# Routing streamed with the base weights in 274-column passes, x2 split straight from PSUM, a new order of the LayerNorm work in the down loop and behind it

## The chip, the cores and the metric

The kernel runs on one core of a Trainium2 chip. The metric is the device time of one execution in microseconds (us). Work is spread over five engines that each run their own instruction list in order: TensorE (PE in the rows; its weight loads are PEld), VectorE (DVE), ScalarE (ACT), GpSimd (POOL) and SyncE (SP), which here issues DMA transfers. Engines wait for each other through semaphores.

## The reference

One decoder layer over 8 sequences of 128 tokens with 512 features. The part that the change touches is the last one: a down projection, a LayerNorm, attention over a context, a LayerNorm, a mixture of four LoRA experts and a last LayerNorm. Mamba mixing and the gate and up projections come before it and stay as they are.

```python
h = h + mamba2(rmsnorm(h))                     # not touched
hid = silu(n @ gate_w.T) * (n @ up_w.T)        # n = rmsnorm(h), 1792 wide
x1 = layernorm(h + hid @ down_w.T)             # LayerNorm 0, "u1"
a  = softmax(x1 @ ctx.T) @ ctx
x2 = layernorm(x1 + a)                         # LayerNorm 1, "u2"
logits = x2 @ gate.T + expert_bias             # 4 experts
e = argmax(logits)
y = x2 @ W_up + (x2 @ lora_A[e].T) @ lora_B[e].T
out = layernorm(x2 + y)                        # LayerNorm 2, "u3"
```

## The kernel before

A tile is one sequence of 128 tokens, so there are 8 tiles. Products that need near-float32 accuracy run as three passes of rounded float32 ("fp32r"): each operand is split in a high part (a rounding copy) and a low part (operand minus high part), and `three_pass` multiplies high by low, high by high and low by high. Its three matmuls are lines L582 to L584 in the rows. Matmuls on plain float32 operands show as two instructions each.

The last stage is a software pipeline, `tail(t)`, written out by hand on each engine. In `tail(t)` TensorE computes the down projection of tile t (14 blocks of three passes, `down`, cut in segments by `SEGS`), and between the segments it serves tile t-1 (transposing u1 in `turn_x1`, scores in `attend`, transposing the softmax in `turn_ex`, `mix` with the context) and tile t-2 (transposing u2 in `turn_x2`, `route`, `base`, `turn_z`, `lora`). `route` multiplies x2 by 36 columns (4 gate columns and 4 x 8 LoRA columns) in plain float32; `base` multiplies it by the 512 columns of W_up, 4 blocks of three 512-column passes; `lora` adds the chosen expert's product into the same bank of PSUM.

VectorE in `tail(t)` adds u1 of tile t-1 and takes its moments, does the same for u3 of tile t-3, normalises both, splits x2 of tile t-2, takes the row maximum of the scores, computes the low part of the next tile's hidden rows (`split_hid`, 1792 columns), picks the expert (`route`, eight small instructions that depend on each other), and forms and normalises u2. ScalarE copies the transposes from PSUM, makes the high part of the hidden rows, the exponentials, and the two small steps (`rstd`) between moments and normalising. The order on each engine is the order of the code. Tiles 0 to 2 run from straight code, tiles 3 to 6 in a loop with two tiles a round, and tile 7 (`last`) in an order of its own with `END_SEGS`, behind which tiles 5, 6 and 7 drain.

Down, loop and end wait for these semaphores: `hid_lo` (low part of hidden rows there), `q_ok` (x1 transposed and copied), `x2_lo`, `ex_ok`, `zm_ok`, `zmT_ok`, `ln_out` and `route_ps`.

## Time and profile before

| what | value |
|---|---|
| median of 3 runs | 414.51 us (412.84, 414.51, 414.68) |
| the profiled execution | 412.89 us |
| its span, first to last instruction | 411.2 us |
| TensorE busy | 97% of the span |
| VectorE, ScalarE busy | 71%, 46% |
| mean granted TensorE clock | 0.992 of full |

The span is the stretch that the rows below are timed in, from 0 at its start. The profiled execution's own time is 1.69 us longer than the span. Of the three runs one is at the profiled execution's time and two are 1.6 to 1.8 us above it.

### The profile page before, as it was taken

To read this page: it belongs to the slowest core of one execution; us is meant where nothing else is said; L and a number is where in the kernel's file an instruction comes from. 1 tells how busy PE (TensorE), PEld (TensorE's weight loads), DVE (VectorE), ACT (ScalarE), POOL (GpSimd) and SP (SyncE) were. 2 spreads that over 40 slices of the span, in tenths; PEclk is the share of its full clock that TensorE was granted. 3 is DMA by queue.
4 is the path that set the end of the run, shared out by engine and by line. 5 is a ranking of instruction groups with operands and counts; after the bars stand their busy time and mean duration, and the time that the engine had idled before them with its cause. 6 is when DMAs were issued, how large, how long until landed. Compare 5 with 4: busy or idle time off the path is not lost.

```text
span 411.2 us, 5381 instructions
## 1 busy us (share of the span) xinstructions
PE 398.0 (97%) x1932; PEld 318.5 (77%) x1936; DVE 290.3 (71%) x517; ACT 190.0 (46%) x383; POOL 131.6 (32%) x117
## 2 busy tenths in 40 slices
PE   7999999999999999999999999999999999999984
PEld 3878887766669997888888888887888788787753
DVE  3496991146886689889897989695567657675676
ACT  6668745736655555443515242863314133142131
POOL 3404225614424663565564737740000000000000
PEclk9899999999999999999999999999999999999998
DMA  7901111010000105111112031352110120110002
GB/s 248 316 2 52 53 51 51 2 51 2 0 1 2 52 2 205 53 51 53 51 51 68 36 102 52 110 184 66 51 53 26 52 78 26 51 47 29 28 0 77
DMA packets 11659, 25.52 MB, mean 62 GB/s; under 512 B 1681, under 2 KB 1809, under 8 KB 11634
## 3 DMA queue, kind: packets, MB, share of 16 engines
q1 hardware_dynamic: 10482, 23.10, 16.9%
q10 hardware_dynamic: 1152, 2.10, 1.4%
q8 instruction: 14, 0.23, 0.2%
q14 instruction: 11, 0.09, 0.1%
HBM read 23.10 MB, written 2.10 MB: 61 GB/s over the span
## 4 chain that ended last, share of the span: by engine, by line
PE 85%; DVE 7%; ACT 3%; POOL 2%; issue 2%; ACTq 0%; DVEq 0%; POOLq 0%
PE bank L582 23%; PE bank L584 23%; PE bank L583 23%; PE bank L653 2%; PE bank L707 2%; PE bank L640 2%; PE bank L847 2%; PE bank L858 1%; PE bank L593 1%; PE bank L869 1%; POOL sets L501 1%; PE bank L621 1%; DVE tmp L1668 1%; PE bank L662 1%; DVE big L1459 1%
## 5 line engine op out<-in xcount | busy, mean ns | idle before, releaser
L582 PE MATMUL bank<-sets,station 128*128 128x512 f32 (+1 forms) x424 | 164.1, 387 | 1.1 <-DVE station L1549 0.7
L584 PE MATMUL bank<-sets,station 128*128 128x512 f32 (+1 forms) x424 | 158.5, 374 | 0.0
L583 PE MATMUL bank<-sets,station 128*128 128x512 f32 (+1 forms) x424 | 158.3, 373 | 0.0
L582 PEld LDWEIGHTS bank<-sets,station 128*128 128x128 f32 x424 | 80.0, 189 | 18.6 <-issue 3.6
L583 PEld LDWEIGHTS bank<-sets,station 128*128 128x128 f32 x424 | 80.0, 189 | 15.3 <-issue 2.2
L584 PEld LDWEIGHTS bank<-sets,station 128*128 128x128 f32 x424 | 79.8, 188 | 14.4
L540 POOL TENSOR_TENSOR big<-tmp,side_f 128x512 f32<-128x512 f32 x17 | 26.4, 1568 | 23.8 <-DVE side_f L1555 23.8
L1425 DVE SCALAR_TENSOR_TENSOR big<-bank,cw,big 128x508 f32<-128x508 f32 (+2 forms) x36 | 26.2, 739 | 5.1 <-ACT big L1026 4.2
L462 POOL TENSOR_TENSOR station<-raw,station 128x1024 fp32r<-128x1024 f32 x7 | 16.8, 2395 | 40.3 <-ACT station L968 40.3
L1269 ACT ACTIVATE small<-small 128x1 f32<-128x1 f32 x24 | 7.0, 294 | 47.9 <-DVE small L1670 47.9
L1555 DVE TENSOR_TENSOR side_f<-side_f,bank 128x512 f32<-128x512 f32 x36 | 24.5, 683 | 4.0 <-PE bank L584 3.6
L1539 DVE TENSOR_TENSOR station<-raw,station 128x512 fp32r<-128x512 f32 (+1 forms) x24 | 20.9, 909 | 6.1 <-ACT station L1164 6.1
L1459 DVE SCALAR_TENSOR_TENSOR big<-bank,xb,big 128x128 f32<-128x128 f32 x32 | 9.0, 343 | 19.4 <-ACT big L1048 19.4
L1555 DVE TENSOR_TENSOR tmp<-tmp,bank 128x512 f32<-128x512 f32 x30 | 20.3, 681 | 2.8 <-PE bank L584 2.7
L1549 DVE TENSOR_TENSOR station<-side_f,station 128x512 fp32r<-128x512 f32 x24 | 19.4, 817 | 3.2 <-ACT station L1187 3.2
L1164 ACT ACTIVATE station<-raw 128x512 fp32r<-128x512 f32 x12 | 7.5, 623 | 29.6 <-PE bank L584 29.6
L493 POOL TENSOR_TENSOR big<-big 128x512 f32<-128x512 f32 x8 | 10.2, 1281 | 29.7 <-DVE big L1459 29.7
L1187 ACT ACTIVATE station<-side_f 128x1024 fp32r<-128x1024 f32 x12 | 12.7, 1059 | 14.2 <-POOL side_f L532 14.2
L1675 DVE TENSOR_SCALAR tmp<-tmp,small 128x512 f32<-128x512 f32 x24 | 12.9, 538 | 7.6 <-ACT small L1271 7.6
L1668 DVE BATCH_NORM_STATS2 tmp<-tmp 128x6 f32<-128x512 f32 x24 | 16.7, 695 | 0.8
L1741 DVE SCALAR_TENSOR_TENSOR tmp<-bank,small,tmp 128x512 f32<-128x512 f32 x8 | 6.0, 750 | 14.3 <-PE bank L858 14.2
L527 POOL TENSOR_TENSOR side_f<-raw 128x256 f32<-128x256 f32 x12 | 9.1, 754 | 20.3 <-DVE station L1549 20.3
(182 smaller groups left out, 672.0 us busy)
## 6 DMA issues: line engine op xcount, KB each, us to landing
raw<-wstream SPq DMA_DIRECT2D x31, 512.0 KB, 3.4
rows<-x SPq DMA_DIRECT2D x8, 256.0 KB, 4.7
big<-ctxT SPq DMA_DIRECT2D x8, 256.0 KB, 2.8
big<-ctx SPq DMA_DIRECT2D x8, 256.0 KB, 3.0
out<-tmp ACTq DMA_DIRECT2D x8, 256.0 KB, 2.0
big<-ln_w SPq DMA_DIRECT2D x1, 256.0 KB, 5.5
big<-lora_b SPq DMA_DIRECT2D x3, 64.0 KB, 5.2
ga<-gate_lora SPq DMA_DIRECT2D x1, 72.0 KB, 5.4
```

The costliest lines, as they stand in the source:

```text
L462: pool.tensor_tensor(dst, raw[:, raw_slot(n), :], hi.bitcast(F32), ALU.subtract).then_inc(w_lo, 1)
L540: pool.tensor_tensor(hid_block(m, hf), blocks(sg[:, k, :]), blocks(value), ALU.mult).then_inc(up_ok, 1)
L582: pe.matmul(ps, a_hi, b_lo, start=first, stop=False)
L583: pe.matmul(ps, a_hi, b_hi, start=False, stop=False)
L584: return pe.matmul(ps, a_lo, b_hi, start=False, stop=last)
L1425: v.scalar_tensor_tensor(out=dst[:, :, s:L], in0=src[:, :, 0:L - s], scalar=cw[:, m, 3 - s:4 - s], in1=dst[:, :, s:L], op0=ALU.mult, op1=A ...
L1459: v.scalar_tensor_tensor(out=dec[:, b % 2, h, :], in0=bank[6][:, bass.ts(h, L)], scalar=xb[:, b % 2, P + H + h:P + H + h + 1], in1=dec[:, ...
L1539: v.tensor_tensor(groupS[:, buf, 1, lo:hi], src, groupS[:, buf, 0, lo:hi].bitcast(F32), ALU.subtract) \
L1549: v.tensor_tensor(groupS[:, buf, 1, q], sums[:, bass.ts(k, D)], groupS[:, buf, 0, q].bitcast(F32), ALU.subtract).then_inc(g_lo, 1)
L1555: v.tensor_tensor(dst, other, product_bank(g, n), op).then_inc(done, 1)
L1668: v.bn_stats(stats[:, k, :], u).then_inc(ln_st[i], 1)
L1675: v.tensor_scalar(u, u, mv[:, k, 0:1], lrs[:, k:k + 1], ALU.subtract, ALU.mult).then_inc(ln_out[i], 1)
```

## The change

The two-part weights of `base` become rows of 548 columns: the 36 routing columns stand in front of the 512 columns of W_up, and are split in high and low parts like them. `base_half` runs the 548 columns as two products of 274 columns, in banks 7 and 6, 12 passes each; the first holds the routing result, and `route` as a product of its own is gone but for the last tile. `lora` writes into both banks, with 238 and 274 columns. ScalarE writes the high part of x2 straight from PSUM and VectorE subtracts it from PSUM; the plain copy `x2T` and one VectorE cast are gone. The expert pick is one VectorE instruction shorter. `down` has one segment more, and its third segment stands ahead of `base` and `turn_ex`. VectorE takes u3's moments behind `normed(0)` and `split_hid` behind `route`; ScalarE's `split_hid` stands behind the copies of the transposes. Behind the loop the segments, the order of the drain and the banks are new, the stores of tiles 5 and 6 are issued by SyncE, and the last store is cut in two halves on two queues.

```diff
+ROUTE = E + E * RANK
+BASE_N = D + ROUTE
+PAIR_N = BASE_N // 2
...
-SEGS = ((0, 8), (8, 10), (10, 12), (12, 14))
-END_SEGS = ((0, 8), (8, 9), (9, 10), (10, 11), (11, 14))
+SEGS = ((0, 8), (8, 10), (10, 12), (12, 13), (13, 14))
+END_SEGS = ((0, 5), (5, 6), (6, 8), (8, 9), (9, 13), (13, 14))
...
-        x2S = rawS[:, CH:2 * CH].rearrange("p (s n) -> p s n", s=2)
+        baseS = side_t[:, 0:(2 * DC - 1) * BASE_N].rearrange("p (k n) -> p k n", n=BASE_N)
+        base_end = rawS[:, 2 * CH:2 * CH + BASE_N]
+        x2_parts = (rawS[:, CH:2 * CH].rearrange("p (s n) -> p s n", s=2),
+                    rawS[:, 3 * CH:4 * CH].rearrange("p (s n) -> p s n", s=2))
+        x2S = x2_parts[0]
...
-            sp.wait_ge(stored, 16 * B)
+            last = B - 1
+            sp.wait_ge(ln_out[2], last - 1)
+            sp.dma_start(out[last - 2], u3).then_inc(stored, 16)
+            sp.wait_ge(ln_out[2], last)
+            sp.dma_start(out[last - 1], u1).then_inc(stored, 16)
+            sp.wait_ge(ln_out[2], last + 2)
+            sp.dma_start(out[last, :, HALF_K:D], u_last[:, HALF_K:D]).then_inc(stored, 16)
+            sp.wait_ge(stored, 16 * (B + 1))
...
+                    if halves and c == DC - 1:
+                        turn_z(t - 2, bk=2)
...
+            def route_last(t):
+                pe.wait_ge(ln_u[2], t - 1)
+                pe.wait_ge(x2_ok, 2)
                 for c in range(DC):
-                    mm = pe.matmul(bank[bk][:, 0:E + E * RANK], x2T[:, bass.ts(c, P)], ga[:, c, :],
+                    mm = pe.matmul(bank[7][:, 0:ROUTE], x2T[:, bass.ts(c, P)], ga[:, c, :],
                                    start=(c == 0), stop=(c == DC - 1))
                 mm.then_inc(route_ps, 1)
 
-            def base(t, first_use=False, bk=6, halves=False):
+            def base_last(t, chunks):
+                for c in chunks:
+
+                    pe.wait_ge(x2_lo, t + 1 + c // 2)
+                    q = bass.ts(c, P)
+                    three_pass(pe, bank[6][:, :], x2S[:, 0, q], x2S[:, 1, q], base_w(0, c)[:, ROUTE:BASE_N],
+                               base_w(1, c)[:, ROUTE:BASE_N], c == 0, False)
+
+            def base_half(h, bk, x2, chunks=range(DC)):
+                cols = (slice(0, PAIR_N), slice(PAIR_N, BASE_N))[h]
+                for c in chunks:
+                    q = bass.ts(c, P)
+                    mm = three_pass(pe, bank[bk][:, 0:PAIR_N], x2[:, 0, q], x2[:, 1, q], base_w(0, c)[:, cols],
+                                    base_w(1, c)[:, cols], c == 0, h == 0 and c == DC - 1)
+                    if h == 0 and c == DC - 1:
+                        mm.then_inc(route_ps, 1)
+
+            def base(t, first_use=False):
+
                 pe.wait_ge(x2_lo, t + 1)
                 if first_use:
-                    pe.wait_ge(bw_lo, 2)
-                elif bk == 6:
+                    pe.wait_ge(bw_lo, 5)
+                else:
                     pe.wait_ge(ln_u[2], t)
-                for c in range(DC):
-
-                    if halves and c == 2:
-                        pe.wait_ge(x2_lo, t + 2)
-                    q, k = bass.ts(c, P), bass.ts(c, D)
-                    three_pass(pe, bank[bk][:, :], x2S[:, 0, q], x2S[:, 1, q], sideS[:, 0, k], sideS[:, 1, k],
-                               c == 0, False)
-
-            def turn_z(t):
+                base_half(0, 7, x2S)
+                base_half(1, 6, x2S)
+
+            def turn_z(t, bk=3):
                 pe.wait_ge(zm_ok, t + 1)
-                pe.transpose(bank[7][:, P:2 * P], zm, ident[:, :]).then_inc(zmT_ps, 1)
-
-            def lora(t, bk=6):
+                pe.transpose(bank[bk][:, 0:P], zm, ident[:, :]).then_inc(zmT_ps, 1)
+
+            def lora(t, bks=(7, 6)):
+
                 pe.wait_ge(zmT_ok, t + 1)
-                pe.matmul(bank[bk][:, :], zmT[:, :], lbS[:, :], start=False, stop=True).then_inc(ffn_ps, 1)
+                n = PAIR_N - ROUTE
+                pe.matmul(bank[bks[0]][:, ROUTE:PAIR_N], zmT[:, :], lbS[:, 0:n], start=False, stop=True,
+                          skip_group_check=True)
+                pe.matmul(bank[bks[1]][:, 0:PAIR_N], zmT[:, :], lbS[:, n:D], start=False, stop=True).then_inc(ffn_ps, 1)
+
+            def lora_last(t):
...
+                if d:
+                    down(t, par, 2, first_d)
                 if f:
-                    route(t - 2)
                     base(t - 2, first_f)
                 if a:
                     turn_ex(t - 1)
                 if d:
-                    down(t, par, 2, first_d)
+                    down(t, par, 3, first_d)
                 if f:
                     turn_z(t - 2)
                 if a:
                     mix(t - 1)
                 if d:
-                    down(t, par, 3, first_d)
+                    down(t, par, 4, first_d)
                 if f:
                     lora(t - 2)
...
-            route(last - 2)
+            turn_x2(last - 1, 0)
+            down(last, 1, 5, False, END_SEGS)
             base(last - 2)
-            turn_x2(last - 1, 0)
-            turn_halves(last, u1, ln_out[0], (2, 0), q_ps)
-            turn_z(last - 2)
+            turn_halves(last, u1, ln_out[0], (2, 5), q_ps)
             attend(last, 1, halves=True)
             lora(last - 2)
+            pe.wait_ge(x2_lo, last)
+            base_half(0, 1, x2_parts[1], (0, 1))
             turn_ex(last)
-            route(last - 1)
+            base_half(0, 1, x2_parts[1], (2,))
             mix(last)
-            base(last - 1)
+            base_half(0, 1, x2_parts[1], (3,))
+            base_half(1, 0, x2_parts[1])
+            keep_warm(4, 4, wd(0, 0)[:, 0:P], wd(0, 0))
             turn_halves(last, u2[:, 1, :], ln_out[1], (3, 5), x2_ps)
-            keep_warm(4, 2, wd(0, 0)[:, 0:P], wd(0, 0))
-            turn_z(last - 1)
-            route(last, bk=1, halves=True)
-            lora(last - 1)
-            base(last, bk=0, halves=True)
-            turn_z(last)
-            lora(last, bk=0)
+            route_last(last)
+            turn_z(last - 1, bk=4)
+            base_last(last, (0, 1))
+            lora(last - 1, (1, 0))
+            base_last(last, (2, 3))
+            turn_z(last, bk=4)
+            lora_last(last)
...
-            def copy_x2(t):
+            def hi_of_x2(t, x2=x2S):
                 act.wait_ge(x2_ps, t + 1)
-                act.activation(x2T, bank[3][:, :], ACT.Copy).then_inc(x2_ok, 1)
+                act.activation(x2[:, 0, :], bank[3][:, :], ACT.Copy).then_inc(x2_hi, 1)
...
-                if split:
-                    split_hid(t + 1, 1 - par, first_split)
                 if a:
                     copy_q(t - 1)
                 if f:
-                    copy_x2(t - 2)
+                    hi_of_x2(t - 2)
+                if split:
+                    split_hid(t + 1, 1 - par, first_split)
...
+            def route_low():
+                v.wait_ge(bw_hi, 3)
+                v.tensor_tensor(baseS[:, DC:2 * DC - 1, 0:ROUTE], ga[:, 0:DC - 1, :],
+                                baseS[:, 0:DC - 1, 0:ROUTE].bitcast(F32), ALU.subtract).then_inc(bw_lo, 1)
+                v.tensor_tensor(base_end[:, 0:ROUTE], ga[:, DC - 1, :], baseS[:, DC - 1, 0:ROUTE].bitcast(F32),
+                                ALU.subtract).then_inc(bw_lo, 1)
...
-                v.wait_ge(lg_step, 5 * t + 4)
-                v.tensor_scalar(lg[:, 2, :], lg[:, 1, :], gm[:, 1:2], None, ALU.is_equal).then_inc(lg_step, 1)
-                v.wait_ge(lg_step, 5 * t + 5)
+                v.wait_ge(lg_step, 4 * t + 4)
                 er = E * RANK
                 z = zm[:, 3 * er:4 * er]
-                v.tensor_tensor(z.rearrange("p (e r) -> p e r", e=E),
-                                bank[bk][:, E:E + er].rearrange("p (e r) -> p e r", e=E),
-                                lg[:, 2, :].unsqueeze(2).broadcast_to([P, E, RANK]), ALU.mult).then_inc(z_step, 1)
+                v.scalar_tensor_tensor(out=z.rearrange("p (e r) -> p e r", e=E),
+                                       in0=lg[:, 1, :].unsqueeze(2).broadcast_to([P, E, RANK]), scalar=gm[:, 1:2],
+                                       in1=bank[bk][:, E:E + er].rearrange("p (e r) -> p e r", e=E),
+                                       op0=ALU.is_equal, op1=ALU.mult).then_inc(z_step, 1)
...
-                v.tensor_tensor(u, bank[bk][:, :], u2[:, par, :], ALU.add).then_inc(ln_u[2], 1)
-
-            def split_x2(t):
-                v.wait_ge(x2_ok, t + 1)
-                v.tensor_copy(x2S[:, 0, :], x2T).then_inc(x2_hi, 1)
+                n = PAIR_N - ROUTE
+                v.tensor_tensor(u[:, 0:n], bank[bks[0]][:, ROUTE:PAIR_N], u2[:, par, 0:n], ALU.add)
+                v.tensor_tensor(u[:, n:D], bank[bks[1]][:, 0:PAIR_N], u2[:, par, n:D], ALU.add).then_inc(ln_u[2], 1)
+
+            def add_ffn_last(t, par, u):
+                v.wait_ge(ffn_ps, t + 1)
+                v.tensor_tensor(u, bank[6][:, :], u2[:, par, :], ALU.add).then_inc(ln_u[2], 1)
+
+            def lo_of_x2(t, x2=x2S):
                 v.wait_ge(x2_hi, t + 1)
-                v.tensor_tensor(x2S[:, 1, :], x2T, x2S[:, 0, :].bitcast(F32), ALU.subtract).then_inc(x2_lo, 1)
-
-            def split_halves(t):
+                v.tensor_tensor(x2[:, 1, :], bank[3][:, :], x2[:, 0, :].bitcast(F32), ALU.subtract).then_inc(x2_lo, 1)
...
-                    moments(2, t - 3, u3)
                 if a:
                     normed(0, t - 1, u1)
                 if g:
+                    moments(2, t - 3, u3)
                     normed(2, t - 3, u3)
                 if f:
-                    split_x2(t - 2)
+                    lo_of_x2(t - 2)
                 if a:
                     row_max(t - 1)
+                if f:
+                    route(t - 2)
                 if split:
                     split_hid(t + 1, 1 - par)
```

On TensorE, in `tail(2)` (the loop's tiles are alike), from the scores of tile 1 (L847, L867) on; `x2_lo` is the wait of `base`. Before:

```order
L847 MATMUL bank<-big,tmp 128x128 [waits ctx_in1,q_ok]
L847 MATMUL bank<-big,tmp 128x128 x3
L869 MATMUL bank<-ga,tmp 128x36 [waits x2_ok]
L869 MATMUL bank<-ga,tmp 128x36 x3
L582 MATMUL bank<-side,rawS 128x512 [waits bw_lo,x2_lo]
L583 MATMUL bank<-side,rawS 128x512
L584 MATMUL bank<-side,rawS 128x512
```

and in the changed kernel:

```order
L867 MATMUL bank<-big,tmp 128x128 [waits ctx_in1,q_ok]
L867 MATMUL bank<-big,tmp 128x128 x3
L600 MATMUL bank<-sets,station 128x512
L601 MATMUL bank<-sets,station 128x512
L602 MATMUL bank<-sets,station 128x512
L600 MATMUL bank<-sets,station 128x512
L601 MATMUL bank<-sets,station 128x512
L602 MATMUL bank<-sets,station 128x512
L600 MATMUL bank<-side,rawS 128x274 [waits bw_lo,x2_lo]
```

The 36-column product is gone, six passes of the down projection (L600 to L602 on `sets`) stand between the scores and what follows them, and the base passes have 274 columns.

On VectorE, in a tile of the loop, from the add of u3 (L1714, L1788) to its normalising. Before:

```order
L1714 TENSOR_TENSOR tmp<-bank,tmp 128x512 [waits stored,ffn_ps]
L1668 BN_STATS tmp<-tmp 128x6 [waits ln3_u]
L1670 BN_AGGR small<-tmp 128x2 [waits ln3_st]
L1675 TENSOR_SCALAR tmp<-tmp,small 128x512 [waits ln1_rs]
L1675 TENSOR_SCALAR tmp<-tmp,small 128x512 [waits ln3_rs]
```

and in the changed kernel:

```order
L1788 TENSOR_TENSOR tmp<-bank,tmp 128x238 [waits stored,ffn_ps]
L1789 TENSOR_TENSOR tmp<-bank,tmp 128x274
L1742 TENSOR_SCALAR tmp<-tmp,small 128x512 [waits ln1_rs]
L1735 BN_STATS tmp<-tmp 128x6 [waits ln3_u]
L1737 BN_AGGR small<-tmp 128x2 [waits ln3_st]
L1742 TENSOR_SCALAR tmp<-tmp,small 128x512 [waits ln3_rs]
```

Normalising u1 (the one that waits `ln1_rs`) now stands ahead of u3's moments, and u3's add is two instructions.

On VectorE, further on in the same tile, from the split of x2 to the next tile's hidden rows (L1662, L1729) and the expert pick (from L1680, L1747, on). Before:

```order
L1718 CAST rawS<-tmp 128x512 [waits x2_ok]
L1720 TENSOR_TENSOR rawS<-tmp,rawS 128x512 [waits x2_hi]
L1733 TENSOR_REDUCE small<-bank 128x1 [waits sc_ps]
L1662 TENSOR_TENSOR station<-big,station 128x1792 [waits hid_hi]
L1680 TENSOR_TENSOR tmp<-bank,eb 128x4 [waits route_ps]
```

and in the changed kernel:

```order
L1797 TENSOR_TENSOR rawS<-bank,rawS 128x512 [waits x2_hi]
L1808 TENSOR_REDUCE small<-bank 128x1 [waits sc_ps]
L1747 TENSOR_TENSOR tmp<-bank,eb 128x4 [waits route_ps]
L1749 TENSOR_REDUCE small<-tmp 128x1 [waits lg_step]
L1751 SCALAR_TENSOR_TENSOR tmp<-tmp,small,codes 128x4 [waits lg_step]
L1757 TENSOR_REDUCE small<-tmp 128x1 [waits lg_step]
L1761 SCALAR_TENSOR_TENSOR tmp<-tmp,small,bank 128x32 [waits lg_step]
L1767 CAST tmp<-tmp 128x2x32 [waits z_step]
L1770 TENSOR_TENSOR tmp<-tmp 128x32 [waits z_step]
L1729 TENSOR_TENSOR station<-big,station 128x1792 [waits hid_hi]
```

The 1792-column subtraction is now queued behind the expert pick, which waits for the first half of the base passes.

## Rows read from the trace of the kernel before

**Rows 1.** The page: span, and busy time of an engine, share, instructions

```profile
span 411.2 us, 5381 instructions
PE 398.0 (97%) x1932; PEld 318.5 (77%) x1936; DVE 290.3 (71%) x517; ACT 190.0 (46%) x383; POOL 131.6 (32%) x117
```

**Rows 2.** Windows: length, busy by engine (instructions), granted clock, DMA share, GB/s

```profile
278.00:288.00 10.00, 9.13 (x47) 7.28 (x46) 5.66 (x9) 3.30 (x7) 0.00 (x0) 1.00 0.19 54
288.00:341.00 53.00, 53.00 (x266) 43.30 (x266) 33.57 (x76) 15.16 (x39) 0.00 (x0) 1.00 0.16 50
...
405.70:411.20 5.50, 0.00 (x0) 0.00 (x0) 2.53 (x5) 0.75 (x4) 0.00 (x0) 0.74 0.26 97
```

**Rows 3.** Chain that ended last, one loop tile: start, length, engine, tile, line

```profile
329.87 0.43 PE bank L829 x4
...
332.13 0.89 PE bank L847 x8
333.02 0.82 PE bank L869 x8
333.84 0.31 PE bank L582
...
336.65 0.11 PE bank L853
...
340.50 0.23 PE bank L893
...
346.20 0.44 PE bank L829 x4
```

**Rows 4.** Timeline, TensorE, 256-column fp32r passes: first, last, what follows

```profile
128.81 0.28 PE L582 MATMUL bank<-sets,station 128*128 128x256 f32 x1
...
131.56 0.28 PE L584 MATMUL bank<-sets,station 128*128 128x256 f32 x1
131.68 0.60 PE L684 MATMUL bank<-ident,tmp 128*128 128x128 f32 x4
```

**Rows 5.** Timeline, `tail(1)`: row maximum, and the transpose behind the softmax

```profile
286.92 0.29 DVE L1733 TENSOR_REDUCE small<-bank 128x1 f32<-128x128 f32 x1 [3.67 <-PE bank L847]
...
287.75 0.33 PE L853 MATMUL bank<-ident,tmp 128*128 128x128 f32 x1 [0.87 <-ACT tmp L1293]
```

**Rows 6.** Timeline, VectorE in the loop tile of rows 3

```profile
333.27 2.02 DVE L1662 TENSOR_TENSOR station<-big,station 128x1792 fp32r<-128x1792 f32 x1
...
335.20 0.15 DVE L1680 TENSOR_TENSOR tmp<-bank,eb 128x4 f32<-128x4 f32 x1
...
336.75 0.20 DVE L1701 TENSOR_TENSOR tmp<-tmp 128x32 fp32r<-128x32 f32 x1
...
339.23 0.75 DVE L1741 SCALAR_TENSOR_TENSOR tmp<-bank,small,tmp 128x512 f32<-128x512 f32 x1 [2.21 <-PE bank L858]
...
344.24 0.69 DVE L1668 BATCH_NORM_STATS2 tmp<-tmp 128x6 f32<-128x512 f32 x1
...
345.06 0.52 DVE L1675 TENSOR_SCALAR tmp<-tmp,small 128x512 f32<-128x512 f32 x1
```

**Rows 7.** Chain and timeline: start of tile 7, and the drain behind it

```profile
373.42 0.24 PE bank L582
...
387.15 0.68 DVE L1706 TENSOR_TENSOR tmp<-bank,rows 128x512 f32<-128x512 f32 x1
...
391.63 0.33 PE L889 MATMUL bank<-ident,tmp 128*128 128x128 f32 x1 [0.79 <-DVE tmp L1701]
...
400.65 0.98 PE L869 MATMUL bank<-ga,tmp 128*128 128x36 f32 x8
...
407.92 0.55 DVE L1675 TENSOR_SCALAR tmp<-tmp,small 128x512 f32<-128x512 f32 x1 [0.17 <-ACT small L1271]
```

**Rows 8.** Source view of the store's line L1275

```profile
DMA to landing us min/median/max: 2.0/2.0/2.3
```

**Rows 9.** Lines by form: a VectorE subtraction of 256 columns, busy, mean ns

```profile
L1728 DVE TENSOR_TENSOR rawS<-tmp,rawS 128x256 fp32r<-128x256 f32 x2 | 0.8, 424 | 0.1
```

104 lines of the change are left out of this document (64 added, 40 removed).

## Prediction

> **What bounds the kernel now.** I read the page first, then the windows by stage, then the chain of waits through one tile, and the timeline where an engine waits. The page has TensorE busy for 97% of the 411.2 us span [rows 1], so time can only be won by taking TensorE work away, or from the 3% in which it waits. The windows say where these lie [rows 2]: in the loop over tiles, from 288 to 341 us, TensorE is busy for 53.00 of 53.00 us at full granted clock; from 278 to 288, in `tail(1)`, it is idle for 0.87 us; and in the last 5.50 us it does nothing while VectorE, ScalarE and the last store finish. So there are three kinds of places. In the loop every TensorE nanosecond counts and nothing else does, as long as the other engines keep up. In `tail(1)` a wait can be filled. Behind the loop a chain of small steps across engines counts.
>
> The chain through a loop tile gives the prices [rows 3]. A tile takes 346.20 - 329.87 = 16.33 us, all of it TensorE. The routing product starts at 333.02 and the base passes end at 336.65, where the softmax transpose starts: 3.63 us for the two. Of that 0.82 is routing, the first base pass behind this plain float32 product takes 0.31, and the other eleven take (336.65 - 333.84 - 0.31) / 11 = 0.2273 each. The `lora` pass takes 0.23.
>
> **The change, step by step.** *Base and routing together.* 24 passes of 274 columns replace 12 of 512 and the routing product. No pass of 274 columns is in the trace. The nearest rows are 24 passes of 256 columns, back to back, each with its own weight load: they start at 128.81 and give way at 131.68, so 2.87 / 24 = 0.1196 us each [rows 4]. With the 512-column pass at 0.2273, a column costs (0.2273 - 0.1196) / 256 = 0.42 ns, and 274 columns 0.1196 + 18 x 0.00042 = 0.1272. The bounds are the two rows: 0.1196 at least, 0.2273 at most; I take 0.1272, since 274 is 18 columns from one row and 238 from the other. 24 of them take 3.05 us. The extra 0.08 of the first pass behind a plain float32 product doesn't vanish: it moves to the down pass that now follows the scores. `lora` in two passes takes 0.1196 - 18 x 0.00042 = 0.112 for 238 columns (0.10 at least, which is what one of routing's eight narrow instructions takes, 0.82 / 8 [rows 3]) and 0.127 for 274: 0.24 instead of 0.23. A tile saves 3.63 - 3.05 - 0.08 - 0.01 = 0.49 us. Five tiles (0 to 4) pass through `tail(2)` to `tail(6)`: **2.45 us**. With the pass at 0.1196 they would save 0.9 more.
>
> The Trainium skill (TensorE: Matmul & The Clock Gate, section Back-to-back issue gap) puts the gap between warm matmuls at N / 2.4 + 2.5 ns, which is 117 ns for 274 columns. The rows disagree at 256 columns, where it gives 109 and they show 119.6; the measurement decides. By the page's figure, an estimate, 24 passes would take 2.80 us and the five tiles would save 1.2 us more.
>
> *Tail(1).* Before, the softmax transpose of tile 0 follows the scores at once and waits 0.87 us for the exponentials [rows 5]. Now six down passes stand between, 6 x 0.2273 + 0.08 = 1.44 us, more than the wait. The gain is the 0.87 and part of the slower restart (0.33 for that transpose, 0.11 in the loop [rows 3, 5]): **0.95 us**. Against it stand the new low parts of the weights on VectorE, split in more and smaller instructions ahead of tile 0's LayerNorm. At the price of a 256-column subtraction [rows 9] two more would delay it by up to 0.8, by their widths (108 and 36 columns) by about 0.4. I take nothing, since TensorE has the first eight down blocks of tile 1 to do meanwhile; without that cover it costs up to 0.4.
>
> *Does VectorE keep up?* Here is the work that hides, and it gets less room. Let T be the start of a tile's down passes. TensorE then reaches the end of the first 274-column half after 24 x 0.2273 + 0.87 (two transposes) + 1.36 + 0.89 + 1.44 + 1.53 = 11.55, and VectorE starts the expert pick at about T + 11.75. The pick took 1.74 (335.20 to 336.95 [rows 6]) and has one of eight instructions less, 1.5. Only then comes the subtraction of the next tile's hidden rows, 2.02 [rows 6], which ends at T + 15.3. The next tile starts at T + 16.33 - 0.49 = T + 15.84, and its first pass waits for that subtraction. Slack: 0.5 us; before, the subtraction was done at 335.29, more than 5 us ahead. Next is `normed(0)`: from the start of u2 at 339.23 to the end of `normed(0)` at 345.58 VectorE and ScalarE took 6.35 us [rows 6]. u3's moments, 345.06 - 344.24 = 0.82, now come behind it, and the add in two pieces costs 0.1 more (two of 0.42 [rows 9], little overlapping, for one 512-column add of 0.68 like that in rows 7). So T + 15.3 + 5.65 = T + 20.95, and the transpose that waits for it comes at T + 15.84 + 5.46 = T + 21.3. Slack: 0.35 us. Both hold, so I price this at nothing. Queued behind these two waits is all of TensorE, so a miss shows at once.
>
> *Split of x2 from PSUM, one cast and one pick instruction less.* They shorten VectorE's and ScalarE's lists off the bound; nothing in the loop beyond the slack above.
>
> *The end.* From the first down pass of tile 7 (373.42) to the end of the last normalising (408.47) it is 35.05 us [rows 7]. Three legs: to u1 of tile 7 at 387.15 (13.73), on to the last routing at 400.65 (13.50), and 7.82 to the end. In the first leg u1 of tile 7 started right behind `normed(1)` of tile 6 before. Now the last down block stands behind the transpose that waits for this `normed(1)`: 0.44 + 3 x 0.2273 + about 0.3 of hand-overs, 1.4 to 1.6 us later. The short first segment (5 blocks, 3.4 us) also lets TensorE wait some 1.6 us for `normed(0)` of tile 6, but the transpose then comes no later than before. In the second leg base of tile 5 is 0.58 cheaper with its routing, the routing of tile 6 (0.82) is gone, the 0.79 us wait of `turn_z` [rows 7] is partly covered since it now stands inside the scores (-0.5), and tile 6's 24 half passes cost 0.32 more than 12 whole ones: about 1.6 less. The third leg has the same passes, an add in two pieces and a normalising in two pieces: +0.2. The sum is 0.0 to +0.3; I take a **loss of 0.2**. The last store took 2.0 us to land [rows 8]. Half its bytes on each of two queues saves between 0 and 1.0; I take 0, since the normalising in two pieces (2 x 0.42 by rows 9, for 0.55) gives some back.
>
> The sum: 2.45 + 0.95 - 0.2 = **3.2 us** less. The profiled execution would go from 412.89 to 409.7. The three runs lie at 412.84 and at 414.5 to 414.7, so the median of the changed kernel is 409.7 or, from 414.51, 411.3; I give the middle, 410.6.
>
> **The rivals.** (a) *The narrow pass is slow.* The 238-column `lora` pass is the only fp32r pass under 256 columns, and no row shows one. If it ran at plain float32's price, 0.89 / 4 for 128 columns [rows 3], it would cost 0.41 instead of 0.11: six on the path, 1.8 us, which leaves 1.4. For it: nothing but the missing row; against it: columns are priced alike from 256 to 512. Time about 412.3. (b) *The end gets longer.* It now has more waits of TensorE for VectorE in a row, and u1 of tile 7 is later; 1 to 2.5 us lost leave 0.7 to 2.2: about 412.2. (c) *VectorE becomes the bound of the loop.* The two slacks, 0.35 and 0.5, are small; if both engines' hand-overs eat them and 0.3 more per tile, five tiles give back 1.5, and 1.7 is left: about 412. (d) *Slower: the 274-column pass costs more than its columns.* Its rows of weights are 548 columns apart, so they start at other addresses than those of rows 4, and there are 162 of them on the path (24 for each of tiles 0 to 5, 18 for tile 6). At 0.147 each, the 3.2 us are gone; at 0.160 the kernel is 2 us slower, about 413 by the profile, 416 by the median. For it: only that no such pass was seen; against it: 36-, 128-, 256- and 512-column passes all run at their columns' or their weight load's price. (e) *More gain:* the end gets shorter by a microsecond, as the 0.79 and other waits of the drain are filled: 409.6.
>
> **How the numbers follow.** My forecast 0.55, (a) 0.12, (b) 0.12, (c) 0.06, (d) 0.06, (e) 0.09. Half a percent, 2.07 us, is about what a measurement of this kernel can tell from no change. My forecast (2.3 to 4.1 less, by the bounds of the pass and the end) and (e) are faster, 0.62, and some of (b) and (c), 0.06: 0.68. Most of (a), (b) and (c), and a little of (d), lie within half a percent: 0.26. Slower is (d), 0.06. The range runs from (e) on the lower level of the runs, 412.9 - 4.2 = 408.7, to the weakest of (b) on the upper, 414.5 - 1.0 = 413.5.
>
> **What would show it.** Right: base passes that start 0.127 us apart; a loop tile of 15.85 us; TensorE without idle time from 284 us to the first transposes of tile 7; no wait ahead of L873 in `tail(1)`; the end at 35.0 to 35.3 us from tile 7's first pass. Wrong: a wait of the first down pass for `hid_lo`, or of `turn_x1` for `normed(0)`, in the loop (c); `lora` taking 0.5 (a); passes 0.14 apart or more (d); the end at 36 us or more (b).

## The result, and the profile after

The changed kernel takes 410.44 us (median of 6 runs, 409.62 to 411.23), beside 413.44 us for the kernel before (6 runs, 412.84 to 414.68): a ratio of 0.992, with an interval of 0.990 to 0.995. The profiled execution takes 409.80 us with a span of 408.0, against 412.89 and 411.2. Forecast were 410.6, and 409.7 for a profiled execution. Three of the six runs lie at 409.6 to 409.8 and three at 411.1 to 411.2, so the median falls between them, where no run lies.

First the chain of waits through a loop tile, the answer to [rows 3] (start in us, length, engine, tile, line):

```profile
327.92 0.44 PE bank L847 x4
...
330.18 0.89 PE bank L867 x8
331.07 0.23 PE bank L600
...
332.45 0.13 PE bank L600
...
335.39 0.13 PE bank L602
335.52 0.11 PE bank L873
...
337.99 0.11 PE bank L929
338.10 0.13 PE bank L931
...
343.69 0.44 PE bank L847 x4
```

A tile takes 343.69 - 327.92 = 15.77 us. Four of them, from 296.39 to 359.45, take 63.06, 15.765 each; before, 297.18 to 362.53, 16.34. The 24 passes of base and routing take 335.52 - 332.45 = 3.07 us, 0.128 each, where 0.1272 was forecast. By the figure of the Trainium skill (TensorE: Matmul & The Clock Gate, section Back-to-back issue gap), 117 ns for 274 columns, they would take 2.80, an estimate; the trace stays above it. The page gives that figure for a matmul by itself, without its weight load, and each of these passes has its own. The 238-column `lora` pass (L929) takes 0.11. The down pass behind the scores (L600 at 331.07) takes 0.23.

The windows, as in [rows 2] (busy time of PE, PEld, DVE, ACT and POOL, then the granted clock):

```profile
278.00:288.00 10.00, 10.00 (x51) 8.11 (x50) 6.02 (x12) 3.80 (x8) 0.00 (x0) 1.00 0.20 58
288.00:341.00 53.00, 53.00 (x289) 44.73 (x288) 33.65 (x74) 15.59 (x40) 0.00 (x0) 1.00 0.16 50
```

The 0.87 us wait of [rows 5] in `tail(1)` is gone. VectorE in the same loop tile, by the timeline:

```profile
334.02 0.16 DVE L1747 TENSOR_TENSOR tmp<-bank,eb 128x4 f32<-128x4 f32 x1 [2.62 <-PE bank L602]
...
335.48 2.02 DVE L1729 TENSOR_TENSOR station<-big,station 128x1792 fp32r<-128x1792 f32 x1
...
342.60 0.55 DVE L1742 TENSOR_SCALAR tmp<-tmp,small 128x512 f32<-128x512 f32 x1
```

`normed(0)` (L1742) ends at 343.15, and the transposes that need it start at 343.53 in the same timeline (343.69 in the chain, which starts a piece where the one before it gives way): 0.38 us of slack, forecast 0.35. The next tile's hidden rows are ready at 337.50, 0.6 us before their first pass (forecast 0.5). All of TensorE's waits from 278 us to the end (us in total, times, longest):

```profile
PE bank L847 <- DVE tmp L1742: 1.5, 1, 1.5
PE bank L890 <- ACT tmp L1339: 0.6, 1, 0.6
PE bank L935 <- ACT zmT L1350: 0.4, 1, 0.4
PE bank L883 <- DVE tmp L1742: 0.3, 1, 0.3
PE bank L867 <- ACT tmp L1339: 0.3, 1, 0.3
PE bank L854 <- DVE tmp L1742: 0.2, 1, 0.2
```

All six lie behind the loop. The first is new, and so are some rows of the timeline there, which answer to [rows 7] (the line ahead of them is tile 7's first pass in the kernel before, in the same view):

```profile
373.26 0.40 PE L582 MATMUL bank<-sets,station 128*128 128x512 f32 x1
```

```profile
369.60 0.40 PE L600 MATMUL bank<-sets,station 128*128 128x512 f32 x1
...
374.73 0.66 PE L847 MATMUL bank<-ident,tmp 128*128 128x128 f32 x4 [1.55 <-DVE tmp L1742]
...
385.20 0.69 DVE L1779 TENSOR_TENSOR tmp<-bank,rows 128x512 f32<-128x512 f32 x1 [1.45 <-PE bank L602]
...
397.53 1.05 PE L890 MATMUL bank<-ga,tmp 128*128 128x36 f32 x8 [0.62 <-ACT tmp L1339]
...
404.99 0.74 DVE L1894 TENSOR_SCALAR tmp<-tmp,small 128x256 f32<-128x256 f32 x2 [0.17 <-ACT small L1321]
```

From tile 7's first pass to the last VectorE end this is 405.73 - 369.60 = 36.13 us, against 408.47 - 373.26 = 35.21 before by the same view (the chain of [rows 7] has that pass at 373.42, 0.16 later; so the forecast's 35.05). By the prediction's three legs (to u1 of tile 7, on to the last routing, to the end) it is 15.60, 12.33 and 8.20 us, against 13.89, 13.50 and 7.82 before. The sum by pieces, all measured in the two profiled executions:

| piece | forecast | measured |
| --- | --- | --- |
| up to the first transposes of `tail(1)` (284.17, now 284.44) | 0 | +0.27 |
| `tail(1)`, first transposes to those of tile 1 (13.01, now 11.95) | -0.95 | -1.06 |
| five loop tiles | 5 x -0.49 = -2.45 | 5 x -0.573 = -2.87 |
| the end, tile 7's first pass to the last VectorE end | +0.2 | +0.92 |
| from there to the end of the span (2.73, now 2.27) | 0 | -0.46 |
| sum | -3.2 | -3.2 |

The sum is right, and its terms are wrong against each other. The experiments ask which edit is worth what.

### The profile page after: what moved, and what is told of

It reads as the page before. It is cut to its first block, busy times and chain, and to the rows that moved or that the text cites. A ratio compares the mean times of both kernels' runs of the same rounds, so it can differ in the third digit from the quotient of the medians.

```text
span 408.0 us, 5451 instructions
## 1 busy us (share of the span) xinstructions
PE 394.0 (97%) x1967; PEld 318.5 (78%) x1971; DVE 287.5 (70%) x511; ACT 190.7 (47%) x386; POOL 131.7 (32%) x117
## 4 chain that ended last, share of the span: by engine, by line
PE 82%; DVE 8%; ACT 3%; POOL 2%; issue 2%; DMA 1%; SPq 0%; DVEq 0%; ACTq 0%; POOLq 0%
PE bank L600 23%; PE bank L602 23%; PE bank L601 23%; PE bank L671 2%; PE bank L867 2%; PE bank L658 2%; PE bank L878 2%; DMA rows<-x 1%; POOL sets L519 1%; DVE tmp L1735 1%; PE bank L639 1%; PE bank L680 1%; DVE big L1512 1%; PE bank L883 1%; PE bank L611 1%
## 5 line engine op out<-in xcount | busy, mean ns | idle before, releaser
L600 PE MATMUL bank<-sets,station 128*128 128x512 f32 (+1 forms) x424 | 164.6, 388 | 1.1 <-DVE station L1602 0.7
L602 PE MATMUL bank<-sets,station 128*128 128x512 f32 (+1 forms) x424 | 158.5, 374 | 0.0
L600 PEld LDWEIGHTS bank<-sets,station 128*128 128x128 f32 x424 | 79.9, 189 | 18.0 <-issue 3.6
L602 PEld LDWEIGHTS bank<-sets,station 128*128 128x128 f32 x424 | 79.8, 188 | 14.2
L1742 DVE TENSOR_SCALAR tmp<-tmp,small 128x512 f32<-128x512 f32 x23 | 12.4, 545 | 8.6 <-ACT small L1321 8.4
L602 PE MATMUL bank<-side,rawS 128*128 128x274 f32 (+1 forms) x60 | 17.8, 297 | 0.0
L601 PE MATMUL bank<-side,rawS 128*128 128x274 f32 (+1 forms) x60 | 17.8, 296 | 0.0
```

What stands on the lines that cost most here:

```text
L600: pe.matmul(ps, a_hi, b_lo, start=first, stop=False)
L601: pe.matmul(ps, a_hi, b_hi, start=False, stop=False)
L602: return pe.matmul(ps, a_lo, b_hi, start=False, stop=last)
```

## Experiments

The first 15 us differ by up to 2.1 us between the profiled executions, in rows that no edit touches (last section). So beside each median stands the time in the profiled execution from the first transposes of `tail(1)` (L847 or L829, "x4") to the end of the span, called **the rest** here; it leaves that difference out. It is read from one execution of each kernel, and to about 0.05 us, since spans are given to 0.1. The loop tile is the mean of four tiles, or, where the first of them has no wait yet (e1, e2, e6, e10), of the three behind it.

| kernel | median us (runs) | span | the rest | loop tile |
| --- | --- | --- | --- | --- |
| before | 412.9 to 413.8 (four sets) | 411.2 | 127.03 | 16.34 |
| after | 410.44 (6) | 408.0 | 123.56 | 15.77 |
| e1, before with the segments alone | 414.49 (12) | 412.7 | 128.30 | 16.86 |
| e6, and the LayerNorm order | 415.63 (7) | 414.2 | 129.66 | 17.25 |
| e9, and ScalarE's order | 411.56 (12) | 411.7 | 125.84 | 16.33 |
| e2, after with the old LayerNorm order | 412.65 (12) | 411.8 | 125.95 | 16.37 |
| e10, after with ScalarE's old order | 415.51 (10) | 413.9 | 128.03 | 16.85 |
| e7, after with the old segments | 409.78 (6) | 408.0 | 123.75 | 15.77 |
| e3, after with one store | 410.34 (6) | 409.4 | 123.53 | 15.77 |
| e4, after, down block first | 409.89 (6) | 407.1 | 123.12 | 15.77 |
| e5, after, hidden rows first | 409.54 (6) | 407.3 | 123.36 | 15.77 |
| e8, after with a new end | 407.69 (6) | 405.6 | 121.85 | 15.77 |
| e11, e8 with the old segments | 408.13 (5) | 406.4 | 122.53 | 15.79 |
| e12, e8 with 8 blocks first | 407.32 (4) | 405.6 | 121.72 | 15.77 |

**e1: the order of segments alone.** In the kernel before, `SEGS` and `tail` on TensorE as in the change, and nothing else (the segments behind are numbered on):

```diff
-SEGS = ((0, 8), (8, 10), (10, 12), (12, 14))
+SEGS = ((0, 8), (8, 10), (10, 12), (12, 13), (13, 14))
...
                     attend(t - 1, 1 - par)
+                if d:
+                    down(t, par, 2, first_d)
                 if f:
                     route(t - 2)
                     base(t - 2, first_f)
...
```

> The kernel before with the new order of segments alone: six down passes stand between the scores and the routing, and routing and base stay as they were. Theory: the gain of tail(1) is the order's alone and comes whole, 0.9 to 1.1 us, with no wait at the softmax transpose of tile 0; the first base pass keeps its 0.31 us, since it still follows the 36-column product, and the down pass that now follows the 128-column scores takes 0.23, so a loop tile stays at 16.33 us; the profiled execution goes from 412.9 to about 411.9. Rival, which is the step of the prediction: any fp32r pass behind a plain float32 product takes 0.08 more, so the down pass behind the scores takes 0.31 too, a loop tile 16.41, and five tiles give back 0.4 of the gain. Second rival: the order alone carries most of the 3 us (the wait was the cost, not the columns), about 410.3.

All three were wrong: the kernel is 0.4% slower than before (ratio 1.004, 1.002 to 1.006). `tail(1)` gives its 1.07 us (13.01 to 11.94), and each tile from `tail(3)` on takes about 0.5 more. Two pieces of the chain of waits of this kernel, in one tile:

```profile
333.13 0.23 PE bank L582
...
335.32 0.31 PE bank L582
...
345.07 0.70 DVE tmp L1670
345.77 0.02 issue
345.80 0.18 DVE small L1672
345.98 0.45 DVE tmp L1677
346.43 0.04 issue
346.47 0.66 PE bank L829 x4
```

The new order puts one down block (3 passes, 0.68 us) less behind the softmax product, so VectorE's walk from that product to the normalising of u1 (L1677) ends after TensorE wants it. Ahead of L1677 stand u3's moments (L1670 at 345.07), 0.87 us that u1 doesn't need. The first two rows settle a side question: behind the scores (128 columns wide) a pass takes 0.23, behind the routing's 36-column products 0.31. The rival that took the 0.08 along falls.

**e6 and e9: one order more each time.** e6 is e1 with the change's LayerNorm order, `normed(0)` and then `moments(2)` (e2's edit, below, the other way round, and the same in the straight code of tile 7); e9 is e6 with the change's order on ScalarE:

```diff
-                if split:
-                    split_hid(t + 1, 1 - par, first_split)
                 if a:
                     copy_q(t - 1)
                 if f:
                     copy_x2(t - 2)
+                if split:
+                    split_hid(t + 1, 1 - par, first_split)
```

> The kernel before with the new order of segments and, with it, u1's normalising ahead of u3's moments. Theory: the order of segments alone cost 1.3 us because it moves 3 down passes (0.68 us) ahead of the softmax product, so that normalising u1 came 0.3 us too late in each loop tile, and a wait costs 0.2 more at the restart; with the moments (0.87) out of the way the normalising is some 0.5 us early again, loop tiles go back from 16.8 to 16.33 us, and what is left is tail(1)'s gain of 1.07: a profiled execution of 411.5 to 412 (span 410.0 to 410.4). Rival: the lateness comes from the routing, which follows 1.36 us later, not from the LayerNorm order; then tiles stay at 16.8 us, and about 414.4 is the time.

> The kernel before with all three orders and without the streamed routing: the segments, u1's normalising ahead of u3's moments, and on ScalarE the cast of the next hidden rows behind the two copies for TensorE. Theory: with the LayerNorm order alone ScalarE's root for u3 came later, the cast of 1.7 us behind it held up the copy of u1's transposes, and TensorE waited 0.6 to 0.7 us at the scores; with the cast behind the copies nothing waits in the loop, tiles go back to 16.33 us, and tail(1) keeps its 1.07 us. The end before had its first wait filled by 8 down blocks, so that the gain is not eaten there: 411.7 to 412.1 in the profiled execution. Rival: what holds the loop is VectorE's list itself, 1.36 us later at the routing; then tiles stay above 16.6 us and the time at 414 or more.

e6 went the wrong way again, 17.25 us a tile. TensorE no longer waits for `normed(0)`, and waits behind it. By the timelines of TensorE and ScalarE (in brackets the idle time ahead, and what ended it):

```profile
333.00 1.15 PE L847 MATMUL bank<-big,tmp 128*128 x8 [0.60 <-ACT tmp L1281]
...
330.23 0.29 ACT L1271 ACTIVATE small<-small 128x1 f32<-128x1 f32 x1 [1.44 <-DVE small L1672]
330.56 0.20 ACT L1273 ACTIVATE small<-small 128x1 f32<-128x1 f32 x1
330.67 1.70 ACT L1264 ACTIVATE station<-big 128x1792 fp32r x1
...
332.28 0.58 ACT L1281 ACTIVATE tmp<-bank 128x512 f32<-128x512 f32 x1
```

The root for u3 (L1271) now waits for the later moments, the cast of the hidden rows (L1264, 1.70 us) stands behind the root, and the copy of u1's transposes (L1281) behind the cast; the scores need that copy. e9 moves the cast behind the copies, and no wait of TensorE is left between 278 and 372 us:

```profile
314.13 0.44 PE bank L829 x4
...
330.47 0.44 PE bank L829 x4
...
346.80 0.44 PE bank L829 x4
```

16.33 us a tile, and the rest is 1.19 us shorter than before, 1.07 of it in `tail(1)`; the ratio to before is 0.997 (0.996 to 0.999). That is what the three orders win without the streamed routing; the segments alone (e1) or with the LayerNorm order (e6) lose. The changed kernel's rest is 2.28 us shorter than e9's: so much is due to the streamed routing and what else the change has. The split of x2 from PSUM and the shorter pick were not undone by themselves, so what they are worth is not shown.

**e2 and e10: one order less.** From the other side: the changed kernel with `moments(2)` ahead of `normed(0)` in the loop (e2), and with the cast ahead of the two copies on ScalarE (e10, e9's edit the other way round).

```diff
                     add_ffn(t - 3, 1 - par, stored_tiles=None if first_g else t - 3)
+                    moments(2, t - 3, u3)
                 if a:
                     normed(0, t - 1, u1)
                 if g:
-                    moments(2, t - 3, u3)
                     normed(2, t - 3, u3)
```

> The changed kernel with u3's moments ahead of u1's normalising in the loop, as before. Theory: VectorE has 0.38 us of slack at that normalising, the moments take 0.82 to 0.87, so TensorE waits 0.45 to 0.5 ahead of the transposes of u1 in each of the tiles 3 to 6: loop tiles of 16.2 to 16.3 us in place of 15.77, and 1.8 to 2.4 us more in all. Rival: the order of the two does not matter because something else lets go of that transpose (or ScalarE's root is late anyway): tiles of 15.77 us, no change.

> The changed kernel with ScalarE's cast of the next hidden rows ahead of the copies of u1's and u2's transposes, as before. Theory: the copy of u1's transposes waits for the cast, which waits for the root behind u3's late moments; TensorE waits 0.6 to 0.8 us at the scores of the tiles from 2 or 3 on, and the scores take 1.1 to 1.2 us instead of 0.89: loop tiles of 16.5 to 16.8 us, 3.5 to 5 us more in all, 413.5 to 414.8. Rival: in the changed kernel TensorE is 0.57 us earlier with everything, the cast is free to start as soon as the down product of the tile is done, and at most the six passes of slack go: less than 1 us more.

Both theories held, with sizes at the upper end of what they gave or just above: +2.39 and +4.47 us of the rest, tiles of 16.37 and 16.85. TensorE's waits from 296 to 372 us, of e2 and then of e10:

```profile
PE bank L847 <- DVE tmp L1742: 1.6, 4, 0.4
```

```profile
PE bank L867 <- ACT tmp L1329: 3.4, 4, 0.9
```

In e2 the four waits of 0.4 us are about what 0.87 of moments less 0.38 of slack gives (0.49), and a tile pays 16.37 - 15.77 = 0.60: beyond the wait itself some 0.2 us go at the restart, where the four transposes take 0.66 in the chain in place of 0.44.

**e7: the old segments in the changed kernel.** `SEGS` and `tail` on TensorE as before, base straight behind the scores, all else as changed.

```diff
-SEGS = ((0, 8), (8, 10), (10, 12), (12, 13), (13, 14))
+SEGS = ((0, 8), (8, 10), (10, 12), (12, 14))
...
                     attend(t - 1, 1 - par)
-                if d:
-                    down(t, par, 2, first_d)
                 if f:
                     base(t - 2, first_f)
...
```

> The changed kernel with the old order of segments: base follows the scores at once, and the softmax transpose follows base. Theory: TensorE waits for the exponentials of tile 0 in tail(1) again, which costs the 1.06 us that the order had won; the loop tiles stay at 15.77 us, since all passes are the same and none of them follows a narrow plain float32 product; 1.0 to 1.1 us more in all, 410.7 to 410.9 in the profiled execution. Rival: the order also carries part of the loop's gain (base's passes 0.128 us apart only behind fp32r work, or a wait for x2's low part that the six passes had covered): tiles of 15.85 us or more, and 1.5 us more in all.

Both were wrong: the rest is 0.19 us longer, not 1.06, and the span is the same 408.0. The timeline:

```profile
287.84 0.33 PE L873 MATMUL bank<-ident,tmp 128*128 128x128 f32 x1 [0.87 <-ACT tmp L1341]
...
370.49 0.40 PE L600 MATMUL bank<-sets,station 128*128 128x512 f32 x1
...
374.73 0.66 PE L847 MATMUL bank<-ident,tmp 128*128 128x128 f32 x4 [0.65 <-DVE tmp L1740]
```

The wait in `tail(1)` is back, and tile 7 starts at 370.49 in place of 369.60, 0.89 later. Yet the transposes of u1 of tile 6 start at 374.73 in both kernels: the wait ahead of them is 0.65 here and 1.55 in the changed kernel. What lets them go is VectorE's walk from tile 5's softmax product, and the new order has that product one block (0.68 us) later in its tile. So nearly all that the order wins in `tail(1)` is waited for again at this place. Counted from the first transposes of `tail(1)`, it is 1.08 us ahead at tile 7's first pass; 0.68 go to that later product, 0.2 to the subtraction of the hidden rows, which then holds VectorE past the product's end (e5, below), and 0.19 stay. Without the order the end takes 405.71 - 370.49 = 35.22 us, as before (35.21).

**e4, e5 and e3: pieces of the end.** Three edits, in the order of the diffs: e4 puts the last down block of tile 7 ahead of the transposes of tile 6's u2; e5 has `split_hid` ahead of `route` in VectorE's loop; e3 normalises the last tile in one instruction and stores it whole on SP's queue.

```diff
-            turn_x2(last - 1, 0)
             down(last, 1, 5, False, END_SEGS)
+            turn_x2(last - 1, 0)
             base(last - 2)
```

> The changed kernel with the last down block of tile 7 ahead of the transposes of u2 of tile 6, as before, base of tile 5 behind them. Theory: the 0.9 us that the end lost comes from this block, which made u1 of tile 7 late by 1.7 us: the first leg goes back from 15.6 to about 14.2 us, the second gives back some of it since TensorE has less to do while u1 is normalised, and the end is 0.4 to 0.8 us shorter, 409.1 to 409.4 in the profiled execution. Rival: the legs add up to the same, because behind the loop the products of tile 6 have to be done anyway and only change places with the waits: 35.9 to 36.2 us from tile 7's first pass, no change.

```diff
+                if split:
+                    split_hid(t + 1, 1 - par)
                 if f:
                     route(t - 2)
-                if split:
-                    split_hid(t + 1, 1 - par)
```

> The changed kernel with the subtraction of the next tile's hidden rows ahead of the routing on VectorE, as before the change. Theory: in the loop nothing waits for either, so tiles stay at 15.77 us; only tile 6, whose addition of the attention (369.15) starts 0.33 us after its product has ended because the 1.78 us subtraction runs late, gets its first normalising some 0.3 us earlier, and TensorE's 1.55 us wait there shrinks by as much: 0.2 to 0.3 us less in all. Rival: the subtraction in front makes the routing late, `zm` is late for TensorE's transpose of it, and each tile shows a new wait: 0.2 us or more per tile, over 1 us in all.

```diff
-            sp.wait_ge(ln_out[2], last + 2)
-            sp.dma_start(out[last, :, HALF_K:D], u_last[:, HALF_K:D]).then_inc(stored, 16)
...
+            sp.wait_ge(ln_out[2], last + 1)
+            sp.dma_start(out[last], u_last).then_inc(stored, 16)
...
-            act.wait_ge(ln_out[2], last + 1)
-            act.dma_start(out[last, :, 0:HALF_K], u_last[:, 0:HALF_K]).then_inc(stored, 16)
...
+            normed(2, last, u_last, slot=0)
```

> The changed kernel with the last tile normalised in one instruction and stored whole on SP's queue. Theory: two halves on two queues land sooner than one whole store, which is where the 0.46 us behind the last VectorE instruction came from: from its end to the end of the span 2.6 to 2.8 us instead of 2.27; one normalising of 0.55 instead of two with 0.8 gives 0.25 back, so 0.1 to 0.3 us more in all. Rival: landing takes what it takes whatever the size, and the 0.46 is scatter between executions: 2.3 us behind the last VectorE instruction, and the kernel 0.25 us shorter.

e4: the rest is 0.44 us shorter, at the low end of what was expected (the end by itself 0.52). Its legs are 14.67, 12.74 and 8.20 us (15.60, 12.33 and 8.20 in the changed kernel): 0.93 won, 0.41 given back in the second. e5: 0.20 shorter; TensorE's wait at tile 6 shrinks from 1.55 to 1.33. e3: no change (123.53 against 123.56), which neither its theory nor its rival had. Behind the last VectorE end it needs 2.46 us. The nine kernels with two halves on two queues need 2.27 to 2.35, so the halves do land 0.1 to 0.2 sooner, and their two normalisings take 0.74 where one takes 0.55: about as much. The four kernels with one store on ScalarE's queue (before, e1, e6, e9) need 2.60 to 2.73, so the other part of the 0.46 us is no scatter; e3 has its one store on SyncE's queue, but the queue wasn't tried apart.

**e8, e11 and e12: another order behind the loop.** e8 has e5's order, and:

```diff
-END_SEGS = ((0, 5), (5, 6), (6, 8), (8, 9), (9, 13), (13, 14))
+END_SEGS = ((0, 7), (7, 8), (8, 10), (10, 11), (11, 13), (13, 14))
...
-            turn_x2(last - 1, 0)
             down(last, 1, 5, False, END_SEGS)
-            base(last - 2)
+            pe.wait_ge(x2_lo, last - 1)
+            pe.wait_ge(ln_u[2], last - 2)
+            base_half(0, 7, x2S)
+            turn_x2(last - 1, 0)
+            base_half(1, 6, x2S)
```

e11 is e8 with e7's old segments in the loop; e12 is e8 with 8, 1, 1, 1, 2 and 1 blocks:

```diff
-END_SEGS = ((0, 7), (7, 8), (8, 10), (10, 11), (11, 13), (13, 14))
+END_SEGS = ((0, 8), (8, 9), (9, 10), (10, 11), (11, 13), (13, 14))
```

> The changed kernel with another order behind the loop: the segments of tile 7's down passes are 7, 1, 2, 1, 2 and 1 blocks, the transposes of u2 of tile 6 come behind the last of them and between the two halves of tile 5's base, and the hidden rows are subtracted ahead of the routing as in the run before. Theory: the 1.55 us wait at the transposes of u1 of tile 6 goes because 7 blocks, not 5, stand ahead of it, and the half of base covers the hand-over to u2's transposes; the end goes from 36.1 to 34.3 to 35.2 us from tile 7's first pass, and the profiled execution to 408.0 to 409.0. Rival: as with the down block moved alone, each wait that is filled reappears at the next hand-over, and no more than 0.5 us comes of it: 409.3.

> The kernel with the reordered end, with the old order of segments in the loop. Theory: in the changed kernel the 1.06 us that the order of segments won in tail(1) were lost again at the transposes of u1 of tile 6, since the softmax product of each tile comes 0.68 us later and VectorE's chain with it; the reordered end has 7 blocks ahead of these transposes and hardly a wait, so here the old order costs what it should: 0.8 to 1.0 us more than the reordered end alone, 408.2 to 408.4 in the profiled execution. Rival: the order of segments is worth nothing with any end, since the chain through the softmax product of tile 5 decides: 407.4.

> The kernel with the reordered end, with 8, 1, 1, 1, 2 and 1 blocks in place of 7, 1, 2, 1, 2 and 1. Theory: the 0.14 us wait and the slow restart (0.66 for transposes that take 0.44) at u1 of tile 6 go, while the two gaps behind it are still covered: 0.2 to 0.4 us less, 407.0 to 407.2 in the profiled execution. Rival: the copies on ScalarE now come later by the block, the single block ahead of the scores' exponentials is too short, and the wait moves there: 0.2 us more or no change.

e8 beats both kernels: the rest is 1.71 us shorter than in the changed kernel (it holds e5's order, which is worth 0.2 by itself), and the end takes 403.30 - 368.90 = 34.40 us in place of 36.13, as its theory had it. All of its waits from 262 us on:

```profile
PE bank L890 <- ACT tmp L1342: 0.6, 1, 0.6
PE bank L935 <- ACT zmT L1353: 0.4, 1, 0.4
PE bank L854 <- DVE tmp L1745: 0.4, 2, 0.2
PE bank L867 <- ACT tmp L1342: 0.3, 1, 0.3
```

The wait for u1 of tile 6 is now too short for the list (the transposes start at 373.83 in place of 374.73), and with this end the order of segments is worth more: e11, without it, needs 0.68 us more than e8 where e7 needed 0.19 more than the changed kernel. 0.8 to 1.0 was expected; `tail(1)` costs 1.08 more (283.87 to 296.89, against 283.75 to 295.69), and 0.4 still comes back, since the earlier softmax product leaves nothing to wait for at 7 blocks. e12 moves the rest by another 0.13, less than expected and less than these runs can tell. It has the best median: 407.32 us, a ratio to before of 0.986 (0.984 to 0.988).

## Why the prediction came out right, and where it didn't

**The loop tile: right, mis-sized by 0.08.** The step "The extra 0.08 of the first pass behind a plain float32 product doesn't vanish: it moves to the down pass that now follows the scores" failed. The pass behind the scores takes 0.23 with the change and without it (e1); only behind the 36-column routing does it take 0.31. So a tile saves 0.57 and not 0.49. The passes themselves were forecast within 0.001 us, and rivals (a) and (d) fall with the 0.11 and 0.128 of the tile's chain.

**VectorE keeps up: right, but for an order that the prediction left out.** Both slacks were forecast within 0.1 us, and (c) didn't come. u3's moments behind `normed(0)` are a term of its sum (0.82), and e2 bears that out: with the moments back in front, TensorE waits and 2.4 us are lost. ScalarE's new order is in no term of the prediction, and undone it costs 4.5 us (e10). The change's order of segments can't be had without either: without both it made the kernel slower, and with the LayerNorm order alone too (e1, e6).

**`tail(1)`: right in its place, and worth almost nothing.** 1.06 us are won there (forecast 0.95). The step that failed is "The short first segment (5 blocks, 3.4 us) also lets TensorE wait some 1.6 us for `normed(0)` of tile 6, but the transpose then comes no later than before". The wait is there, 1.55 us; but counted from tile 7's first pass the sentence hides that this transpose is bound by VectorE's walk from tile 5's softmax product, which the new order puts 0.68 us later in the tile. Nearly everything won ahead of it is waited for at it. The prediction added the two terms as if they were independent: -0.95 and +0.2. Measured they are -1.06 and +0.92, and e7 shows that they are nearly one and the same microsecond.

The prediction's own sign for rival (b), an end of 36 us or more, came (36.13), though with 0.92 us lost (b) stays short of its 1 to 2.5. By the legs, about +1.5, -1.6 and +0.2 were forecast; measured are +1.71, -1.17 and +0.38. The first leg looks right and isn't: with the old segments (e7: 14.72, 12.30 and 8.20) it is +0.83, so 0.88 of it are the order's and the late block is worth about half of what was put on it. The second leg is 0.4 short of its forecast; which of its terms is off was not measured. Undoing the late block (e4) wins 0.93 in the first leg and 0.52 in the end.

**The store: mis-sized.** 0 was taken from a range of 0 to 1.0; measured are 0.46 behind the last VectorE end. e3 ties 0.1 to 0.2 of it to the halves and shows that the second normalising takes about as much back; what the rest came from stays open.

So the total, 3.2 us, was right because three misses (0.42 in the tiles and 0.11 in `tail(1)`, 0.46 at the store) paid for one in the end (0.72) and for 0.27 at the start. The direction and the tile's gain were earned; that the sum came out to a tenth was luck.

## What to carry to other kernels

A gain ahead of a hand-over counts only as far as the engine on the other side is early there too: before adding up terms, ask of each later wait which chain releases it, and whether the change moves the start of that chain. When the order of one engine's work changes, follow the thing that it now needs earlier through every engine that prepares it, since the work standing ahead of it on each of them may have to move as well; here the order of segments cost 1.3 us alone (e1) and 2.6 with one more order (e6), and the three together won 1.2 (e9). And the last tiles deserve an order of their own, tried on the chip: here a few lines won 1.7 us (e8), beside 2.9 that the change wins in the five loop tiles.

## What the runs showed of the chip that was not expected

**Four profiled executions stay at the lower clock for longer.** In the profiles of e2, e3, e9 and e10 the first transposes of `tail(1)` start at 285.85 to 285.87, in the ten others at 283.75 to 284.54. Two rows of TensorE's timeline, first in the changed kernel, then in e3, which is the same in this stretch:

```profile
4.93 1.12 PE L733 MATMUL bank<-tmp,ones 1*128 1x512 f32 x2
...
8.95 1.91 PE L725 MATMUL bank<-big 128*128 128x512 bf16 x4
```

```profile
5.67 2.07 PE L733 MATMUL bank<-tmp,ones 1*128 1x512 f32 x2
...
10.40 1.91 PE L725 MATMUL bank<-big 128*128 128x512 bf16 x4
```

The product that spreads the LayerNorm weights over the partitions (L733, or L715 in kernels built on the one before) takes 2.07 in exactly these four and 1.12 to 1.43 in the others. It is not alone. Of the ten 512-column passes ahead of it the changed kernel runs the last three 0.25 us apart (4.19 to 4.93), e3 all ten 0.44 apart (1.29 to 5.67). The four passes at L725 above give way after 1.76 us in the changed kernel (at 10.71), where the view has a granted clock of 0.50 from 8 to 10 us, and after 1.71 in e3 (at 12.11), where it has 1.00. e3's eight transposes at 12.11 take 1.70, eight like them at 19.46 take 0.80. So by its rows TensorE was at the lower of its two levels (1.2 and 2.4 GHz) up to about 13.8 us in e3, whatever the view says of that stretch; in the changed kernel it was at the upper one from about 4.2 us, with a fall in between. At the first 256-column passes the two kernels are 1.42 us apart (13.11 and 14.53), at the transposes of `tail(1)` 1.43. Why the clock rises later in the four is open.

**A wait costs more than it lasts.** Behind a wait at full granted clock the four transposes take 0.66 us in the chain for 0.44 (e2), and the scores 1.15 for 0.89 (e6): 0.2 to 0.26 on top of each wait, which is why waits of 0.4 us cost a tile 0.60.
